# Two conditioned transformer layers on one core: where GpSimd splits the MLP weights, how the router's logits are made, and how many row buffers the expert blocks have

## The reference

```
shift_msa, scale_msa, gate_msa, shift_mlp, scale_mlp, gate_mlp = split(silu(c) @ W_ada + b_ada, 6)
x  = x + gate_msa * (attention(modulate(layernorm(x), shift_msa, scale_msa)) @ W_proj + b_proj)
xn = modulate(layernorm(x), shift_mlp, scale_mlp)
# layer 0
x  = x + gate_mlp * (gelu(xn @ W_fc1 + b_fc1) @ W_fc2 + b_fc2)
# layer 1
gate_logits = xn @ w_gate                       # 288 x 4
topk_logits, topk_idx = top_k(gate_logits, 2)
cw  = sum(one_hot(topk_idx, 4) * softmax(topk_logits)[..., None], axis=1)
eo  = gelu(xn @ w1[e] + b1[e]) @ w2[e] + b2[e]  # for each of 4 experts
x   = x + gate_mlp * sum_e cw[:, e] * eo[e]
```

## Time and profile before

| | us |
|---|---|
| median of 3 runs (lowest, highest) | 1669.97 (1665.96, 1670.43) |
| the profiled execution's own time | 1672.97 |
| its span in the profile | 1671.2 |
| PE, PEld busy | 1433.0, 911.0 |
| DVE, ACT, POOL busy | 1140.1, 797.2, 414.6 |
| mean granted clock of PE (share of full speed) | 0.908 |

### The profile page before, as it was taken

How to read it: one execution, slowest core, us unless ns; L and a number is a source line. 1 busy time by engine, 2 the same in 40 slices (tenths; PEclk the granted TensorE clock), 3 DMA queues, 4 the chain that set the end, 5 groups by cost and what they waited for, 6 DMA issues and landing times. The chain is left out here.

```text
span 1671.2 us, 25303 instructions
## 1 busy us (share of the span) xinstructions
PE 1433.0 (86%) x8801; PEld 911.0 (55%) x8801; DVE 1140.1 (68%) x1859; ACT 797.2 (48%) x1554; POOL 414.6 (25%) x485
## 2 busy tenths in 40 slices
PE   4788999999998798697999999997875977999994
PEld 2563333333335587665333333332664876888984
DVE  3648999999945568665899999993543753555653
ACT  0442777777782421252477777777121212222221
POOL 0126321222004227105422222000244341111111
PEclk7895999999999899897699999999865988999997
DMA  6275222222002497037422222000424545665663
GB/s 182 74 201 84 38 37 36 37 45 45 3 3 75 129 298 274 12 118 178 69 45 45 45 45 37 11 3 8 137 101 154 181 125 171 194 206 174 191 206 84
DMA packets 90478, 171.27 MB, mean 102 GB/s; under 512 B 35718, under 2 KB 62280, under 8 KB 87884
## 3 DMA queue, kind: packets, MB, share of 16 engines
q1 hardware_dynamic: 65116, 125.69, 23.6%
q0 software_dynamic: 25248, 44.10, 14.6%
HBM read 114.90 MB, written 55.90 MB: 102 GB/s over the span
## 5 line engine op out<-in xcount | busy, mean ns | idle before, releaser
L822 DVE TENSOR_REDUCE att_neg_max<-att_for_max 128x1 f32<-128x1024 f32 x512 | 601.1, 1219 | 69.6 <-PE att_for_max L897 65.9
L807 ACT ACTIVATE att_probs<-att_scores 128x512 f32<-128x512 f32 x1002 | 522.9, 605 | 208.9 <-PE att_scores L936 208.5
L947 PE MATMUL att_out<-att_probs,V 128*32 128x512 f32 x2048 | 275.4, 610 | 3.9 <-ACT att_probs L807 2.0
L936 PE MATMUL att_scores<-att_QS,att_KS 56*128 56x512 f32 x618 | 226.7, 452 | 18.2 <-ACT att_probs L807 16.1
L897 PE MATMUL att_for_max<-att_KS,att_QS 54*128 54x512 f32 x640 | 241.6, 462 | 0.0
L1883 ACT ACTIVATE experts_gelu<-experts_proj,experts_b 128x256 f32<-128x256 f32 x171 | 81.2, 475 | 266.9 <-PE experts_proj L1983 248.3
L1983 PE MATMUL experts_proj<-experts_x_parts,w_parts 128*128 128x256 f32 (+1 forms) x1197 | 181.1, 293 | 20.8 <-issue 19.4
L936 PEld LDWEIGHTS att_scores<-att_QS,att_KS 56*128 56x128 f32 x618 | 101.1, 184 | 174.2 <-ACT att_probs L807 140.5
L897 PE MATMUL att_for_max<-KS,QS 54*128 54x512 f32 x384 | 165.1, 533 | 17.1 <-PEq L118 8.8
L1983 PEld LDWEIGHTS experts_proj<-experts_x_parts,w_parts 128*128 128x128 f32 (+1 forms) x1197 | 163.4, 198 | 28.2 <-issue 28.0
L1659 DVE CAST perts_hidden_parts<-experts_gelu 128x256 fp32r<-128x256 f32 x171 | 57.6, 337 | 156.8 <-ACT experts_gelu L1883 156.1
(11 more groups left out here) (216 smaller groups left out, 1929.7 us busy)
## 6 DMA issues: line engine op xcount, KB each, us to landing
w_parts<-w_parts SPq DMA_DIRECT2D x19, 2304.0 KB, 9.6
qk_halves<-qkv_qk_parts SPq DMA_DIRECT2D x40, 288.0 KB
slot_rows<-mlp_blank_rows SPq DMA_DIRECT2D x1, 10290.0 KB, 40.5
w_parts<-mlp_next_w_parts SPq DMA_DIRECT2D x16, 576.0 KB, 4.2
att_QS<-qk_halves POOLq DMA_DIRECT2D x120, 72.0 KB, 4.2
att_KS<-qk_halves POOLq DMA_DIRECT2D x60, 144.0 KB, 4.6
w_parts<-w_parts SPq DMA_DIRECT2D x19, 432.0 KB, 10.8
experts_rows<-slot_rows SPq DMA_DIRECT2D x19, 294.0 KB, 2.9
```

Of the source, the lines that this page charges most:

```text
L807: nc.scalar.activation(PR[st % 2][:, j, :], score_bank(st, n), ACT.Exp, scale=SCALE).then_inc(exp_done, 1)
L822: nc.vector.tensor_reduce(negm[half][:, c:c + 1], psM[ring % 2][:].rearrange("p a n -> p (a n)"), AX_X, ALU.max, negate=True).then_inc(rin ...
L936: nc.tensor.matmul(score_bank(st, n), KS[g % SLOTS][rows, p, k * P:(k + 1) * P], QS[g % SLOTS][rows, half, p, :], start=True, stop=True).t ...
L947: last = nc.tensor.matmul(psO[32 * j:32 * j + 32, :], T.V[:, g, k, 32 * j:32 * j + 32], PR[st % 2][:, j, :], start=(k == 0), stop=(k == KT ...
```

## The change

1. **Splitting moves into attention 0.** POOL splits all 30 pieces (6 of layer 0, 24 of the experts) in attention 0, five after each group load from group 2 on (`side_work`), and itself stores the parts in DRAM (`w1_parts`, `w2_parts`). The projection stage loads layer 0's parts, and the last stage loads w2 of all four experts with four transfers of SP at its start. POOL has no split left in the projection stage, in MLP 0 or among the blocks.
2. **Logits as four more columns.** In attention 1 POOL works out, for every row of X and of the gated projection weights, its product with `w_gate` (scaled by the modulation), as 4 extra columns (`router_columns`: one multiplication of 128 x 288 x 4 and a tree of additions; 16 tiles of X and 8 of weights, 4 after each group load, and before them the constants in `router_rows`). The projection then has 292 columns, and the logits follow from them, the mean and the deviation of each row by four small DVE operations. The transposes, ACT's copies and the float32 matmuls of the routing go. The modulation of a row is now one operation each of ACT, DVE and POOL (L1806), before the scatter (L1811).
3. **Row buffers.** Four instead of three: the rows of block b+2 are loaded when the adds of block b-2 have landed. The two adds of one block no longer wait for each other.
4. **MLP 0** is written out over its 36 steps, with five accumulators; the reading and adding of a block happen in steps 1 and 2 of the next one.

The core of the diff:

```diff
...
+            raw_loads, outs = [0], [0, 0]
+
+            def load_piece(n):
+                M, idx, e, kind, k = splits[n]
+                if n:
+                    pool.wait_ge(piece_split, n)
+                if kind == 2:
...
+            def split_piece(n):
...
+                pool.wait_ge(raw_in, 16 * raw_loads[0])
+                if n >= 2:
+                    pool.wait_ge(done, 16 * outs[n % 2])
+                nc.gpsimd.tensor_copy(w[0:r, 0, 0:width], raw[0:r, 0:width]).then_inc(hi_split, 1)
+                pool.wait_ge(hi_split, n + 1)
+                at, lo = (W_LO, 0) if strips else (slice(0, P), 1)
+                nc.gpsimd.tensor_tensor(w[at, lo, 0:width], raw[at, 0:width], w[at, 0, 0:width].bitcast(F32), ALU.subtract
+                                        ).then_inc(piece_split, 1)
+                if n + 1 < len(splits):
+                    load_piece(n + 1)
+                pool.wait_ge(piece_split, n + 1)
+                if strips:
+                    nc.gpsimd.dma_start(T.w1_scr[idx, 0:STACK, STK], w[0:STACK, 0, :].bitcast(F32)).then_inc(done, 16)
+                elif kind == 1:
+                    nc.gpsimd.dma_start(T.w1_scr[idx, :, HI + k], w[:, 0, :].bitcast(F32)).then_inc(done, 16)
+                    nc.gpsimd.dma_start(T.w1_scr[idx, :, LO + k], w[:, 1, :].bitcast(F32)).then_inc(done, 16)
+                else:
+                    nc.gpsimd.dma_start(T.w2_scr[idx, :, :, KC * k:KC * (k + 1), :],
+                                        w[:, :, 0:width].rearrange("p a (f n) -> p a f n", f=KC).bitcast(F32)
+                                        ).then_inc(done, 16)
+                outs[n % 2] += 2 if kind == 1 and not strips else 1
...
+            def router_rows():
...
+                for b in range(B):
+                    row_of = T.mrow[:, 1, b, :].rearrange("p (c o) -> p c o", o=1).broadcast_to([P, C, E])
+                    at = router(nc.gpsimd.tensor_tensor(G[:, b], wgate[:], row_of, ALU.mult))
+                    pool.wait_ge(router_steps, at)
+                    router_sum(G[:, b], None, T.route[:, 0, b, :])
...
+            def router_sum(rows, values, out):
+                else:
+                    at = router(nc.gpsimd.tensor_tensor(prod[:], rows, values, ALU.mult))
+                n = C
+                while n > 1:
+                    half = n // 2
+                    pool.wait_ge(router_steps, at)
+                    at = router(nc.gpsimd.tensor_tensor(prod[:, 0:half, :], prod[:, 0:half, :], prod[:, half:2 * half, :],
+                                                        ALU.add))
...
+                pool.wait_ge(router_steps, at)
+                at = router(nc.gpsimd.tensor_copy(out, prod[:, 0, :]))
...
+            def router_columns(n):
+
+                if n == 0:
+                    router_rows()
+                    pool.wait_ge(wp_gated, B)
+                if n < TILES:
+                    b, ap = n * P // SEQ, T.X[:, n, :]
+                else:
+                    b, ap = (n - TILES) // GPB, T.wp[:, (n - TILES) // GPB, (n - TILES) % GPB, :]
+                values = ap[:, 0:C].rearrange("p (c o) -> p c o", o=1).broadcast_to([P, C, E])
+                router_sum(G[:, b], values, ap[:, C:CE])
+
+            side = len(splits) if splits else TILES + B * GPB
+            per_group = -(-side // (GROUPS - SLOTS + 1))
+
+            def side_work(g):
+
+                for n in range((g - SLOTS + 1) * per_group, min((g - SLOTS + 2) * per_group, side)):
+                    if splits:
+                        split_piece(n)
+                    else:
+                        router_columns(n)
...
+                if g >= SLOTS - 1:
+                    side_work(g)
             pool.wait_ge(wp_gated, B)
+            for n in range(2):
+                if splits:
+                    pool.wait_ge(piece_out[n], 16 * outs[n])
...
         def _(sp):
-            load_expert(sp, S, W, 0, 0)
-            load_biases(sp, W, 0, T.b1[0], T.b2[0], bias_in)
-            sp.wait_ge(bias_in, 32)
...
-            pool.sem_inc(S.w2_split, 1)
-            split_expert(nc, pool, S, T.w1[0], T.w2[0], 0)
+            sp.dma_start(T.w1[:, 0:STK, :].bitcast(F32), T.w1_scr[E, :, 0:STK, :]).then_inc(weights_in, 16)
+            sp.dma_start(T.w1[0:STACK, STK, :].bitcast(F32), T.w1_scr[E, 0:STACK, STK, :]).then_inc(weights_in, 16)
...
-            for n, (e, k) in enumerate(pieces):
-                sp.wait_ge(next_split, n + 1)
...
-                if n + 2 < len(pieces):
-                    load(n + 2)
...
+            for k in range(NBLK * NF):
+                act.wait_ge(h_ready, k + 1)
+                if k >= RING:
+                    act.wait_ge(parts_ready, k - RING + 1)
...
+            def gated(i):
+
+
+                    nc.vector.tensor_tensor(upd[:, t, :], psY[(i * TPB + t) % YB][:, 0:C], T.gate[l][:, 1, i // HALVES, :],
+                                            ALU.mult).then_inc(y_read, 1)
...
+                if i and f == 1:
+                    gated(i - 1)
+                if i and f == 2:
+                    add(i - 1)
...
+            def up(k):
+                i, f = divmod(k, NF)
+                if k >= RING:
+                    pe.wait_ge(gelu_ready, k - RING + 1)
...
                                                                     in1=off[:], op0=ALU.mult, op1=ALU.add))
-                at = route(nc.vector.tensor_scalar(eb[:], eb[:], float(E - 1), None, ALU.min))
-            update(0)
-            modulate(0)
             dve.wait_ge(consts_ready, 1)
             for i in range(NG):
-                if i + 1 < NG:
-                    update(i + 1)
+                update(i)
+                if i:
+                    place(i - 1)
+                scales(i)
                 choose(i)
-                if i + 1 < NG:
-                    modulate(i + 1)
-                place(i)
+            place(NG - 1)
...
             load_w1(T.w1_scr[0], 0)
+            for e in range(E):
+                sp.dma_start(w2all[:, e].bitcast(F32), T.w2_scr[e]).then_inc(w2_in, 16)
...
-            load_rows(2, value(row_of, 2, SLOT_ROWS - EBLK))
+            for b in range(2, XG):
+                load_rows(b, value(row_of, b, SLOT_ROWS - EBLK))
             for b in range(1, EBLOCKS - 1):
                 sp.wait_ge(up_ready, b * NF)
                 load_w1(w1_of(b + 1), (b + 1) % 2)
-                if b + 2 < EBLOCKS:
-                    sp.wait_ge(added_out, 16 * ETILES * b)
+                if b >= 2 and b + 2 < EBLOCKS:
+                    sp.wait_ge(added_out, 16 * ETILES * (b - 1))
                     load_rows(b + 2, value(row_of, b + 2, SLOT_ROWS - EBLK))
...
-            for k in range(KC):
-                load_w2(k)
-                split_w2(k)
             for i, (j0, n) in enumerate(ROUTED):
+                for t in range(n):
+                    pool.wait_ge(scaled, j0 + t + 1)
+                    h = HR[:, j0 + t, 0:C]
+                    nc.gpsimd.tensor_tensor(h, h, T.mrow[:, 0, b, :], ALU.add).then_inc(filled, 1)
                 pool.wait_ge(route_steps, seen["slots", i])
...
-                    if n:
-                        pool.wait_ge(added_out, 16 * n)
+                    if b:
+                        pool.wait_ge(added_out, 16 * ETILES * b)
...
-                e = b + 1
-                if e < E:
-                    for k in range(KC):
-                        load_w2(e * KC + k)
-                        split_w2(e * KC + k)
                 add_out(b)
...
+                if j >= TPB:
+                    pe.wait_ge(added, j - TPB + 1)
+                b, at = divmod(j * P, SEQ)
+                for g in range(GPB):
+                    last = nc.tensor.matmul(psP[j % TPB][:, 0:CE], T.O[:, b * GPB + g, at:at + P], T.wp[:, b, g, :],
+                                            start=(g == 0), stop=(g == GPB - 1))
...
+            for i, (j0, n) in enumerate(ROUTED):
+                for t in range(n):
+                    project(j0 + t)
+                    if i and t == 1:
+                        positions(i - 1)
+            positions(NG - 1)
```

585 lines of the change are left out of this document (238 added, 347 removed).

## The result

The change takes the kernel from 1670.2 us (median of four runs on the same chip) to 1625.09 (1621.28 to 1625.92): ratio 0.9729, interval 0.9706 to 0.9753. That is 45 us less, where 82 were forecast, and 1 us outside the forecast range. The profiled execution has 1625.62, its span is 1623.9. Two executions, one of `inphase` (2980.52 us) and one of the kernel before beside `padded` (4124.73), were far slower than the rest and stand in none of the figures here.

What follows compares the result with a forecast made beforehand. Attention was taken as bound by PE and DVE together, POOL having room, with weak stretches elsewhere. Terms -9.5 - 1.5 + 5 + 9 - 31 - 52 - 3 = -83 on 1672.97 gave 1590, as median 1588; range 1558 to 1624 us.

Steps and rivals of the forecast that it cites:

- Attention 0: Attention 0: POOL's splits hold DVE and their stores share queues with small transfers; +5 us, bounds 0 and +20.
- The test of whether a group load is late: Attention 0: load 7 must start by 419.7, allowing 9.04 us per piece; at 8.0 it fits.
- Transfers beside small transfers: Attention 0: stores of 30 pieces share the queues with small transfers of maxima and inverses; +2 us.
- DVE held by POOL: Attention 0: POOL's splits hold DVE's small operations 5.6 us over 13 spans, about half absorbed by slack; +3 us.
- Rival C: Attentions absorb everything, 14 us less, and routing reaches its better bound, 5 less; 1560 to 1575 us; chance 0.10.
- Attention 1: Attention 1: late load 7 adds 0 to 3 us, held DVE operations +7; +9 us, bounds 0 and +40.
- Rival B: Attention 1: POOL late, a column costing 9 to 10 us, not 8.5; +12 to +37, 1600 to 1625; chance 0.20.
- Rival E: Attention 1: POOL becomes its clock, kernel slower than before; a column must reach 12.2 us; chance 0.03.
- MLP 0: MLP 0: without POOL's splits, PE's waits for DVE and slow steps behind them go; -9.5 us, bounds -5 and -12.
- Routing: Layer 1's projection and routing: POOL becomes the bound, first `up` at 1253; -31 us, bounds -20 and -36.
- rival D: Scatters slow beside the w2 load, or w1 waits stay in the blocks; +10 or +19, 1598 to 1607; chance 0.07.
- Blocks: Expert blocks: waits for rows and w1 go, 16.2 us per block; -52 us, bounds -33 and -57.

Runs made afterwards that it cites:

- inphase: `share01` with POOL's attention 1 router work dealt out anew and the CAST of the inverses' high part replaced by a second RECIPROCAL; ratio 0.9537.
- padded: `inphase` with 8 unused columns behind each third of the pieces' SBUF tiles; median 1590.5 us, ratio 0.9527.
- late4: Kernel before, with four POOL multiplications and no added transfers in front of each load of groups 3 to 7 in attention 0; 1694.53 us.
- late8: Kernel before, with eight POOL multiplications and no added transfers in front of each load of groups 3 to 7 in attention 0; 1682.61 us.
- share0: Changed kernel with attention 0's 30 pieces dealt out as 3, 4, 4, 4, 4, 11 instead of five per group; 1613.75 us, ratio 0.9662.
- share01: `share0` with attention 1's 24 router columns also dealt out, as 0, 4, 4, 4, 4, 8; 1599.61 us, ratio 0.9572.
- apart: Kernel before, with only large transfers added on POOL's queue in attention 0 and only POOL multiplications added in attention 1; 1698.8 us.
- back: Changed kernel with 16 POOL multiplications added in MLP 0, and three row buffers with the old wait for adds in the blocks; 1648.6 us.
- serial4: Changed kernel with a block's two adds again waiting for each other, four row buffers kept; 1635.44 us.

## Why the prediction was wrong

- **Attention 0 (+5 forecast, +40 measured): the step that failed.** The test of whether a group load is late asked only whether it lands before its maxima are computed, and it used nothing but POOL's time. In its own terms it held: load 7 began at 413.22, before the limit of 419.7, and with the forecast's own formula that is a piece of 8.8 us, more than its 8.0 and under the 9.04 that it allowed. But by its own sum load 7 starts at 393.7, 17 us behind the 376.85 of the kernel before, and the forecast put that delay at nothing. A load that is in time for its own use had left its slot, and there it met SP's store of the maxima. `late4` shows this alone at +23, `late8` that twice the delay costs less, `share0` and `share01` that the right slot gives back 21 to 28 in the profiled executions. A third of the 40 us is PE's slower matmuls behind its waits; the forecast had no term for the clock in attention.
- **Transfers beside small transfers (+2 forecast).** What is left with the loads in place is 13 to 20 us, DVE's held operations included. `apart` shows that such transfers alone can cost 24 with PE waiting for maxima. The forecast saw the DMA engines idle in the earlier trace rows and priced by that share; what counts is how late a transfer of a few KB lands. What property of the large ones does it stays open.
- **DVE held by POOL (+3 forecast)** was right in kind. The forecast had 5.6 us of holds in attention 0 and 12.5 in attention 1, half of each absorbed; DVE's busy time rose by 3.2 and 4.3. In `share0` and `share01`, where PE stands less, it rose by 8 to 11 in either. In `apart` 6 us of holds cost attention 1 2.8, so half is borne out once. The row that was to show free reductions, 163.72, overlaps POOL's multiplication only in its last 1.5 us; over whole attentions the reductions keep 1.22. Rival C, that the attentions absorb everything, is out.
- **Attention 1 (+9 forecast, +13.7).** The size is near, the reason was not the forecast's. A column costs 7.43 us, not 8.3 to 8.6, and `router_rows` 32.1, not 36, so load 7 has room. But `router_rows` and four columns stand ahead of one load, and it starts at 918.28, ends beside the store at 925.26, and PE waits 4.11. That span takes 28.2 us, and one more, where load 6 at 1039.94 meets the store at 1043.58, takes 27.0, both at a granted clock of 0.87 to 0.88: 11 of the 13.7 us (timelines of POOL, SP, PE after):

```profile
888.26 2.25 POOL L868 TENSOR_TENSOR att_router_products<-att_router_rows,X 128x1152 f32<-128x1152 f32 x1
890.59 3.92 POOL L873 TENSOR_TENSOR att_router_products<-att_router_products 128x576 f32<-128x576 f32 x6
...
918.28 1.21 POOL L456 DMA_DIRECT2D QS<-qk_halves  x2 [0.37 <-POOL X L880]
...
925.26 2.75 SPq L765 DMA_DIRECT2D att_QS<-att_neg_max_rows  x4
...
934.40 0.79 PE L1072 MATMUL att_scores<-att_QS,att_KS 56*128 56x512 f32 x1 [4.11 <-DMA att_QS<-att_neg_max_rows]
```

  Rival B had a place (POOL late in attention 1) and a total of 1600 to 1625, and 1625.09 lies at its edge, but its price per column was wrong and most of the loss is in attention 0; its time was met by luck. Rival E fell with it.
- **MLP 0** (-9.5, measured -10.4): right. `back` shows that POOL's arithmetic costs this stage more than that even with the written-out loop. What the loop gives by itself was not run.
- **Routing** (-31, measured -29): right. The slots came 28.8 us after the start, not 26; an addition took 0.71, not 0.83, and the first eight scatters were issued 1.3 to 1.5 us apart, like all others, while the DMA engines were at 0.97 to 1.00 with w2's load and what followed it. So rival D's first half is out, and with no wait at `up` its second.
- **Blocks** (-52, measured -58): right in mechanism, the pitch 16.05 against 16.2 forecast. The forecast took the two causes for additive with the buffers as the cure of w1; `serial4` and back's three buffers show that either the fourth buffer or the paired adds is enough.
- **Tail** (-3, measured -4.0): right; serial adds cost 3.1 of it in `serial4`.
- **The range** ended 1 us short because one mechanism, late small transfers, was in none of the cases: +20 was the upper bound of attention 0, from DVE's hold alone.

## What to carry to other kernels

Work put on an idle engine shifts whatever that engine issues next. Before filling a gap, ask not only whether the next transfer still lands in time, but which small, latency-bound transfers of other queues it will now meet, and deal the work out so that the engine waits again before each issue. Where two edits cure one wait, test each alone: here either was enough.

## What the runs showed of the hardware

- Transfers of 4 KB of one queue (the maxima, in four issues) keep PE waiting over 4 us when they meet the eighteen issues of another: 4.19 at 231.70, with the DMA engines at 0.75 in that span, and 4.54 in `late4`, with the engines at 0.25 from 411.5 to 440.2.
- Attention that runs undisturbed has a granted clock of 1.00 from its second span on; in spans in which PE stood some us it is 0.79 to 0.94, and the same matmuls take up to 4 us more. Stands of 1 to 2 us more mostly left it at 1.00 (`late8`).
- The w2 load reached more than the 298 GB/s on which the forecast built; window of the kernel after, columns as above:

```profile
1220.00:1230.00 10.00, 6.51 (x32) 5.02 (x30) 7.98 (x35) 4.41 (x8) 1.86 (x3) 0.98 1.00 428
```

- DVE's RECIPROCAL on 128x16 that writes the high part took 0.19 to 0.20 us in all 30 cases of `inphase`, 21 of them while POOL computed; the subtraction behind it was held up to 1.9.
- A POOL multiplication of 1152 elements whose second input repeats its innermost elements takes 2.25 us, less than the subtraction's 2.62 of the earlier trace rows; one with the same tile as both inputs takes 2.11 (`late4`).
